# Attention row sums: pairs of probability tiles folded into quads by accumulating transfers, half as many ones-matmuls, and a block loop written out

## What is computed

```python
qkv = (h @ Wqkv.T + bqkv).reshape(B, N, num_heads, hd, 3)
...
energy = jnp.einsum('bhqd,bhkd->bhqk', q, k)
att = jax.nn.softmax(energy, axis=-1) / D ** 0.5
out = jnp.einsum('bhqk,bhkd->bhqd', att, v)
```

## Time and profile before

| | us |
|---|---|
| median of three runs | 3467.74 |
| the profiled execution's own time | 3469.48 |
| its span | 3467.7 |
| PE busy | 3200.3 (92%) |
| DVE busy | 2216.4 (64%) |
| POOL busy | 1566.3 (45%) |
| ACT busy | 1527.7 (44%) |
| POOL adds L1711, 256 of 4.583 us | 1173.3 |
| `weigh` matmuls L1565, 4096 records | 547.0 |
| `total` matmuls L1575, 2048 records | 266.6 |
| HBM traffic over the span | 61 GB/s |

### The profile page before, as it was taken

One profiled execution on the slowest core, in us unless ns is written; L12 is line 12 of the kernel. 1 busy time (PEld: TensorE's weight loads), 2 busy tenths in 40 slices (PEclk: granted clock), 3 DMA queues, 4 the chain that ended last, 5 costly groups with the idle time before them and its releaser, 6 DMA issues. The chain is left out here.

```text
span 3467.7 us, 52215 instructions
## 1 busy us (share of the span) xinstructions
PE 3200.3 (92%) x16326; PEld 1973.9 (57%) x16326; DVE 2216.4 (64%) x3513; ACT 1527.7 (44%) x2770; POOL 1566.3 (45%) x538
## 2 busy tenths in 40 slices
PE   4786999999997989899999999999999999999976
PEld 2675777787775767644444444444444444444354
DVE  7885222222214436478888788888787887888458
ACT  2222232322222322355555555555555555556632
POOL 2665211001111110166666666666666665666655
PEclk8887999999998999999999999999999999999988
DMA  6233100000002463511031201122101230100044
GB/s 245 77 110 115 49 22 4 23 24 24 25 13 103 167 191 131 157 27 26 14 74 32 56 14 25 32 56 62 26 13 26 62 74 14 26 13 7 4 162 147
DMA packets 119434, 214.40 MB, mean 62 GB/s; under 512 B 11719, under 2 KB 29147, under 8 KB 118794
## 3 DMA queue, kind: packets, MB, share of 16 engines
q1 hardware_dynamic: 119180, 211.20, 20.3%
HBM read 135.34 MB, written 75.53 MB: 61 GB/s over the span
## 5 line engine op out<-in xcount | busy, mean ns | idle before, releaser
L1711 POOL TENSOR_TENSOR pair<-probs 128x2048 f32<-128x2048 f32 x256 | 1173.3, 4583 | 739.4 <-ACT probs L1650 739.4
L1673 DVE TENSOR_REDUCE part_max<-psum 128x1 f32<-128x512 f32 x1984 | 1227.7, 682 | 334.9 <-PE psum L1540 334.4
L1650 ACT ACTIVATE probs<-psum 128x512 f32<-128x512 f32 x2048 | 1068.6, 602 | 764.5 <-PE psum L1554 763.9
L1540 PE MATMUL psum<-keys,queries 96*128 96x512 f32 x1984 | 833.6, 420 | 5.2 <-DMA queries<-q_parts 5.2
L1554 PE MATMUL psum<-queries,keys 97*128 97x512 f32 x2048 | 794.1, 409 | 40.4 <-ACT probs L1650 28.9
L1540 PEld LDWEIGHTS psum<-keys,queries 96*128 96x128 f32 x1984 | 375.1, 189 | 458.8 <-DVE part_max L1673 375.2
L1565 PE MATMUL psum<-probs,values 128*32 128x512 f32 x4096 | 547.0, 606 | 4.1 <-ACT o_sum L1632 2.9
L1554 PEld LDWEIGHTS psum<-queries,keys 97*128 97x128 f32 x2048 | 381.1, 190 | 245.0 <-ACT probs L1650 176.9
L980 DVE TENSOR_TENSOR h_lo<-w_stage,h_hi 128x512 fp32r<-128x512 f32 x128 | 96.7, 756 | 528.3 <-ACT h_hi L918 528.3
L911 ACT ACTIVATE w_stage<-psum,b_col 128x512 f32<-128x512 f32 x128 | 88.3, 690 | 510.0 <-PE psum L38 510.0
L1024 POOL TENSOR_TENSOR ffn_u_lo<-ffn_u,ffn_u_hi 128x512 fp32r<-128x512 f32 x32 | 41.2, 1287 | 553.9 <-DVE ffn_u_hi L970 553.9
(11 more groups left out here) (305 smaller groups left out, 3734.9 us busy)
## 6 DMA issues: line engine op xcount, KB each, us to landing
queries<-q_parts SPq DMA_DIRECT2D x96, 256.0 KB, 4.8
keys<-k_parts SPq DMA_DIRECT2D x42, 512.0 KB, 7.2
x<-in_x_dram SPq DMA_DIRECT2D x8, 1024.0 KB, 7.9
y<-in_x_dram SPq DMA_DIRECT2D x8, 1024.0 KB, 6.4
y_rows<-y SPq DMA_DIRECT2D x8, 1024.0 KB, 5.1
qkv_z<-z_rows SPq DMA_DIRECT2D x8, 1024.0 KB, 5.5
q_parts<-qk_hi SPq DMA_DIRECT2D x32, 256.0 KB, 2.0
q_parts<-qk_lo SPq DMA_DIRECT2D x32, 256.0 KB, 2.3
```

Of the source, the lines that this page charges most:

```text
L1540: nc.tensor.matmul(psum[:, MX + j % 3, :], queries[n][0:R, h, qt * P:(qt + 1) * P], keys[n // PB][0:R, h, kc * CH:(kc + 1) * CH], start=Tr ...
L1650: act.activation(probs[kt % NPROB][:, h, :], psum[:, SC + unit % 3, :], ACT.Exp).then_inc(exp_ready, 1)
L1673: dve.tensor_reduce(part_max[:, at, kc:kc + 1], psum[:, MX + j % 3, :], AX.X, ALU.max).then_inc(max_read, 1)
L1711: pool.tensor_tensor(pair[p % 2][:, :, :], probs[2 * p % NPROB][:, :, :], probs[(2 * p + 1) % NPROB][:, :, :], ALU.add).then_inc(pair_read ...
```

## The change

`NPROB` goes from 8 to 6 and the number of `pair` buffers from 2 to 4 (`NPAIR`). After every second add, POOL issues a transfer that adds one pair buffer onto the other, 128 x 2048 float32, 1 MiB; a semaphore `folded` counts those that have landed. Four such folds a block. `total` multiplies the folded buffer, four times a block instead of eight, in steps 1, 5, 9 and 13 (`SUM_LAG` 9). ACT copies the sums out after step 5 instead of step 4. `blocks` is a plain Python loop over all 32 blocks, for every engine, and SP's loop over the groups likewise.

```diff
-    NPROB = 8
+    NPROB, NPAIR = 6, 4
+    QUADS = PAIRS // 2
...
-    AV_LAG, SUM_LAG = 2, 5
+    AV_LAG, SUM_LAG = 2, 9
...
-    pair = [sb(f"pair{n}", [P, HG, CH]) for n in range(2)]
+    pair = [sb(f"pair{n}", [P, HG, CH]) for n in range(NPAIR)]
...
-        block(0, 0, True, False)
-        with engine.Fori(0, ITERS - 1) as it:
-            for n in range(1, NB):
-                block(it, n, False, False)
-            block(it + 1, 0, False, False)
-        for n in range(1, NB):
-            block(ITERS - 1, n, False, n == NB - 1)
+        for count in range(NB * ITERS):
+            block(count // NB, count % NB, count == 0, count == NB * ITERS - 1)
...
-            def total(it, n, p):
-
-                pe.wait_ge(pair_ready, PAIRS * (NB * it + n) + p + 1)
-                if p == 0:
+            def total(it, n, r):
+
+                pe.wait_ge(folded, 16 * (QUADS * (NB * it + n) + r + 1))
+                if r == 0:
                     pe.wait_ge(den_copied, NB * it + n + 1)
                 for h in range(HG):
-                    mm = nc.tensor.matmul(psum[h * HD:(h + 1) * HD, DEN, :], ones[:, :], pair[p % 2][:, h, :],
-                                          start=(p == 0), stop=(p == PAIRS - 1))
+                    mm = nc.tensor.matmul(psum[h * HD:(h + 1) * HD, DEN, :], ones[:, :], pair[(2 * r + 1) % NPAIR][:, h, :],
+                                          start=(r == 0), stop=(r == QUADS - 1))
...
-                    if (kt - SUM_LAG) % 2 == 0 and (kt >= SUM_LAG or not first):
-                        total(*pair_of(*lagged(it, n, kt, SUM_LAG)))
+                    if (kt - SUM_LAG) % 4 == 0 and (kt >= SUM_LAG or not first):
+                        total(*quad_of(*lagged(it, n, kt, SUM_LAG)))
...
-                        act.wait_ge(pair_ready, PAIRS * count + (kt - NPROB) // 2 + 1)
+                        act.wait_ge(pair_ready, (tile - NPROB) // 2 + 1)
...
                     pool.wait_ge(exp_ready, 2 * HG * (number + 1))
-                    if p >= 2 or not first:
-                        pool.wait_ge(sums_ready, number - 1)
-                    pool.tensor_tensor(pair[p % 2][:, :, :], probs[2 * p % NPROB][:, :, :], probs[(2 * p + 1) % NPROB][:, :, :],
-                                       ALU.add).then_inc(pair_ready, 1)
+                    quad = QUADS * count + p // 2
+                    if p >= NPAIR or not first:
+                        if p % 2 == 0:
+                            pool.wait_ge(folded, 16 * (quad - 1))
+                        else:
+                            pool.wait_ge(sums_ready, quad - 1)
+                    pool.tensor_tensor(pair[number % NPAIR][:, :, :], probs[2 * number % NPROB][:, :, :],
+                                       probs[(2 * number + 1) % NPROB][:, :, :], ALU.add).then_inc(pair_ready, 1)
+                    if p % 2 == 1:
+
+                        pool.wait_ge(pair_ready, number + 1)
+                        if quad > 0:
+                            pool.wait_ge(folded, 16 * quad)
+                        pool.dma_start(pair[number % NPAIR][:, :, :], pair[(number - 1) % NPAIR][:, :, :],
+                                       accum_op=ALU.add).then_inc(folded, 16)
```

More of the change, by code:

```diff
@@ L1420, in attention_stage @@
     sc_ready, exp_ready = sem("scores_ready"), sem("exp_ready")
[L1421 removed]
+    av_ready, pair_ready, folded, sums_ready = sem("av_ready"), sem("pair_ready"), sem("pairs_folded"), sem("sums_ready")
     max_ready, max_read, turning, neg_ready = (sem(n) for n in ("max_ready", "max_read", "max_turning", "neg_ready"))
@@ L1519, in group @@
                         store(count - 1, g - 1, B - 1, NCH - 1)
[L1521 to L1524, removed]
+            for g in range(NG):
+                group(g, g == 0, g == NG - 1)
             store(B * NCH * NG - 1, NG - 1, B - 1, NCH - 1)
@@ L1551, in score @@
                     pe.wait_ge(exp_ready, NB * UNITS * it + unit - 2)
-                elif not (n == 0 and isinstance(it, int)):
+                elif it > 0:
                     pe.wait_ge(exp_ready, NB * UNITS * it)
@@ L1564, in weigh @@
                 for h in range(HG):
-                    mm = nc.tensor.matmul(psum[h * HD:(h + 1) * HD, OUT, :], values[n // PB][:, kt, h * HD:(h + 1) * HD], probs[kt % NPROB][:, h, :],
+                    mm = nc.tensor.matmul(psum[h * HD:(h + 1) * HD, OUT, :], values[n // PB][:, kt, h * HD:(h + 1) * HD], probs[tile % NPROB][:, h, :],
                                           start=(kt == 0), stop=(kt == NKT - 1))
                 mm.then_inc(av_ready, 1)
-            def total(it, n, p):
-                pe.wait_ge(pair_ready, PAIRS * (NB * it + n) + p + 1)
-                if p == 0:
+            def total(it, n, r):
+                pe.wait_ge(folded, 16 * (QUADS * (NB * it + n) + r + 1))
+                if r == 0:
                     pe.wait_ge(den_copied, NB * it + n + 1)
                 for h in range(HG):
-                    mm = nc.tensor.matmul(psum[h * HD:(h + 1) * HD, DEN, :], ones[:, :], pair[p % 2][:, h, :],
-                                          start=(p == 0), stop=(p == PAIRS - 1))
+                    mm = nc.tensor.matmul(psum[h * HD:(h + 1) * HD, DEN, :], ones[:, :], pair[(2 * r + 1) % NPAIR][:, h, :],
+                                          start=(r == 0), stop=(r == QUADS - 1))
                 mm.then_inc(sums_ready, 1)
@@ L1583, in lagged, with quad_of @@
                 return (it, n - 1, kt + NKT - lag) if n > 0 else (it - 1, NB - 1, kt + NKT - lag)
-            def pair_of(it, n, kt):
-                return it, n, kt // 2
+            def quad_of(it, n, kt):
+                return it, n, kt // 4
             def one(it, n, first, last):
@@ L1619, in _ @@
                 weigh(ITERS - 1, NB - 1, kt - AV_LAG)
-            for kt in range(NKT + 1, NKT + SUM_LAG, 2):
-                total(ITERS - 1, NB - 1, (kt - SUM_LAG) // 2)
+            for kt in range(NKT + 1, NKT + SUM_LAG, 4):
+                total(ITERS - 1, NB - 1, (kt - SUM_LAG) // 4)
         @block.scalar
@@ L1634, in copy_sums @@
             def copy_sums(count):
-                act.wait_ge(sums_ready, PAIRS * (count + 1))
+                act.wait_ge(sums_ready, QUADS * (count + 1))
                 act.activation(den[:, :], psum[:, DEN, :], ACT.Copy).then_inc(den_copied, 1)
@@ L1649, in one @@
                         unit = UNITS * n + HG * kt + h
-                        act.activation(probs[kt % NPROB][:, h, :], psum[:, SC + unit % 3, :], ACT.Exp).then_inc(exp_ready, 1)
+                        act.activation(probs[tile % NPROB][:, h, :], psum[:, SC + unit % 3, :], ACT.Exp).then_inc(exp_ready, 1)
                     if not first:
@@ L1653, in one @@
                             copy_out(count - 1)
-                        if kt == SUM_LAG - 1:
+                        if kt == SUM_LAG - 4:
                             copy_sums(count - 1)
```

## The result

| | before | after |
|---|---|---|
| median of the timed runs | 3468.75 us | 3411.45 us |
| lowest, highest | 3467.65, 3473.09 | 3406.56, 3419.18 |
| the profiled execution's own time | 3469.48 | 3406.56 |
| its span | 3467.7 | 3404.4 |

The ratio is 0.983, with an interval of 0.981 to 0.984: 57 us faster. The forecast was 3352 with a range of 3338 to 3400. The change does what it was said to do, and half of the gain is missing.

The account below looks back on a forecast made before the run. PE was taken to set the pace of the attention blocks. From the profiled 3469.5 us, -110 (totals), -14.7 (loop) and +9 (end) gave 3353.8; with the median 1.7 lower, 3352 us, range 3338 to 3400.

Parts of the forecast that it names:

- Half the totals, 110 us: PE in the blocks: four totals fewer per block, 0.86 us each over 32 blocks, block 57.5 to 54.0 us.
- The loop, 14.7 us: Six back edges of the block loop: straight code removes PE's stops and slow steps, -14.7 us, bounds 0 and -20.9.
- The fold, F = 9 us with its issue: POOL's adding transfer of 1 MiB: 9 us from issue to landing, from 4.3 to 19.2.
- In a block it is hidden. Two limits hold.: Folds inside blocks cost nothing while four in series fit 54.0 us and `total` comes late enough: F up to 13.5.
- The clock: After PE's stop at a back edge, a weigh takes 1.94 us instead of 1.07; straight code takes this away.
- POOL's issues, 1.3 us: Four fold issues per block in POOL's list, 1.3 us each, no cost up to some 3 us.
- the rival of 32 us from it: Folds nearly too slow or POOL too late: DVE starts each block about 1 us late, 3384; 20%, 3367 to 3440.
- Six tiles: zero: ACT's writes to six probability tiles instead of eight: 8.7 us to spare, 5.8 in the last block, no cost.
- The end, +9: Last fold stands between the last add and last `total`: +9 us, from 4.3 to 19.2; PE waits about 12.
- Folds in series: Rival: F above 13.5 us makes POOL, `total` and PE wait, a block takes 4F; 3672 to near 4080, 6%.
- PE or POOL wait for `pair` transfers inside blocks: Sign named to show the prediction wrong: waits of PE or POOL for fold transfers within blocks.

Follow-up runs that it names:

- the run with nothing else: The kernel before with its loops written out and no other change; 3451.5 us, ratio 0.993.
- its own run: Six probability tiles instead of eight, against the kernel before with its loops written out; 3449.4 us, ratio 0.995 to the kernel before.
- the third fold late: Changed kernel with each block's third fold issued one add later and totals two steps later (SUM_LAG 11); 3353.7 us, ratio 0.966.

## Why the prediction was wrong, step by step

- **Half the totals, 110 us.** Right as a size, on PE's path: the steps without `total` are 3.3 us, and where nothing stops PE a block is 53.95 us against the 54.0 forecast. In the changed kernel part of it is given back.
- **The loop, 14.7 us.** Right: 17.0 by the run with nothing else. The edge of the prediction's rows is one of the two worst: PE stands 1.65 to 2.17 us at the six edges, and the clock fell after two of them.
- **The fold, F = 9 us with its issue.** Right in size: 7.2 us from issue to landing, which is 0.87 for the issue and the rest for the transfer. The estimate from the Trainium skill, 6.8, was nearer, and the plain copy's 4.6 stands beside its 4.4. The trace agrees with the Trainium skill in both: "DMA: Bandwidth & Descriptors", section "Anatomy of one DMA — SWDGE (gpsimd) path", for the size of the copy, and "Collectives: The Full Stack", section "The bandwidth ceiling", for the add being slower, here by 2.6 us. That the second read is the reason, as it says of reduce-scatter, no run here shows.
- **"In a block it is hidden. Two limits hold."** This is the step that failed. I counted who waits for the fold, and found room. I did not ask who else's transfer is in flight with it. The prediction says that "nothing else of size is in flight in most blocks"; what counts is not size but a deadline, and the row of maxima has one. It was in the chain from L1055 over L1062 to the first score, with 2.8 us to spare once the `total` of step 15 was gone: the last of the four issues begins at 1767.61; 1.7 us more, the landing in the kernel before, are 1769.4, and PE needs the row at 1772.2. The fold took that and 1.3 us more. So its price inside the blocks, put at nothing, was 57.6 us over 31 of them: 36.8 of stops and 20.8 of slow matmuls.
- **The clock.** Where PE stands for 1.3 us at a block's border, some steps after it run at the lower clock. The prediction had seen this at the loop's edges, and had put it down as a thing of the past; its sum has no term for a new stop.
- **POOL's issues, 1.3 us.** 0.87 measured, covered as said. DVE's product L1685 was not late by it, as the blocks of 53.95 us with all issues in place show, so the rival of 32 us from it did not come. The measured time lies in that rival's range of 3367 to 3440, and the loss sits at the block's start where the rival put it, but it is larger and has another cause: the agreement is luck.
- **Six tiles: zero.** Right, by its own run.
- **The end, +9.** Right: +7.3, PE's wait is 9.9 us where 12 was forecast.
- **Folds in series.** It did not come. The median landing is 7.2 us against a limit of 13.5, but the reserve was not large everywhere: folds issued while the keys, queries and values of a later block are loaded take up to 13.4 us. One add waited for a fold, for 2.0 us, and no `total` inside a block.

Of the signs that were to show it wrong, "PE or POOL wait for `pair` transfers inside blocks" came only in that one wait of POOL, which cost nothing; PE waits for another transfer, and no sign had been named for it. The sign was a poor one besides: with the third fold late POOL waits for a fold in nearly every block, and that kernel runs at the forecast time.

## What to carry to other kernels

When a change adds large transfers, list the small ones that already have a waiter, with issue, landing and deadline, and not only who waits for the new ones: here transfers of 2 KB with less than 3 us to spare cost 57 us beside 1 MiB that had 5 us of its own (the median from the third fold's landing to its `total`). Then move the large one by a step, together with its own deadline, to where its neighbours have room: here the loads of the queries beside it took twice as long and no computing engine waited for them. And where PE is the bound, add to every stop what its clock loses after it, here 21 us on 37.

## What the hardware showed that was not expected

- A fold of 1 MiB with the add lands in 7.2 us, a plain copy in 4.6, a quarter with the add in 3.3: with the add a line through the two is 2.0 us and 5.2 us per MiB. Beside loads of keys, queries and values single folds took up to 13.4.
- Transfers of 2 KB issued from another queue just behind the issue of a fold do not pass it: beside the adding one the last of them lands 0.2 to 0.4 us after it. Medians to landing are 1.7 us alone, 2.6 beside a quarter of a fold, 3.7 beside the plain copy, 5.3 beside the adding one. The one issued 0.2 us ahead of the fold still has a median of 1.7.
- After stops of the same length, 1.2 to 1.4 us, PE's clock fell in 8 blocks of 26, and after all five of 1.7 us and more; but in the kernel before it did not fall after three stops of 1.7 us and one of 2.0 at the loop's edges. What decides this was not tried.
- The stages ahead of the first score, the same code in all kernels, took 1435.3 to 1444.6 us in the profiled executions. Differences of a few microseconds between kernels must be read from the stretch that was changed.
